# A graph kernel's first root product in three fp32r terms, and the last third of three roots between two neighbour sums

## The reference

```
out = x @ W_root + bias
for r in range(NUM_RELATIONS):
    out += (sum of x over the neighbours under relation r / max(degree_r, 1)) @ W_r
```

## Time and profile before

| | |
|---|---|
| median of 3 runs | 801.77 us (800.8 to 802.37) |
| the profiled execution's own time | 805.78 us |
| its span, first to last instruction | 804.0 us |
| mean granted TensorE clock | 0.997 |
| busy: TensorE, DVE, GpSimd, ScalarE | 770.6, 599.6, 490.8, 423.5 us |

### The profile page before, as it was taken

The page is one execution under the profiler, slowest core; times in us unless marked ns, Lnnn a source line. Parts: engine busy times, 40 slices in busy tenths (PEclk is TensorE's granted clock), DMA queues, the critical chain, the costliest instruction groups (busy, mean ns, idle before and its releaser), DMA issues.

```text
span 804.0 us, 10573 instructions
## 1 busy us (share of the span) xinstructions
PE 770.6 (96%) x4182; PEld 640.3 (80%) x4182; DVE 599.6 (75%) x664; ACT 423.5 (53%) x508; POOL 490.8 (61%) x243
## 2 busy tenths in 40 slices
PE   7999999999999999998989999999998999998998
PEld 4668995677666799667657569999998999985897
DVE  8967139999999630999999987555986498567454
ACT  6524456777774442777867734434541454253742
POOL 0534709899998374698999936741873177805500
PEclk9999999999999999999999999999999999999999
DMA  9136427767765463385668838554463445350001
GB/s 359 45 80 235 158 79 198 171 166 209 199 182 130 167 226 118 69 220 105 142 186 201 263 125 303 183 183 164 151 220 134 157 157 202 114 236 0 2 1 40
DMA packets 28585, 126.22 MB, mean 157 GB/s; under 512 B 4084, under 2 KB 6644, under 8 KB 28152
## 3 DMA queue, kind: packets, MB, share of 16 engines
q1 hardware_dynamic: 23240, 104.24, 39.1%
q0 software_dynamic: 4176, 15.21, 10.2%
q10 hardware_dynamic: 1120, 6.10, 2.0%
HBM read 100.63 MB, written 0.79 MB: 126 GB/s over the span
## 4 chain that ended last, share of the span: by engine, by line
PE 70%; DVE 15%; POOL 5%; ACT 4%; DMA 2%; issue 2%; DVEq 0%; SPq 0%; ACTq 0%
PE ps L1156 26%; PE ps L1122 12%; DVE prod L2054 8%; PE ps L1447 6%; PE ps L1187 5%; PE ps L1494 4%; PE ps L1669 3%; ACT prod L868 2%; DVE qi_t L2076 2%; PE ps L1314 2%; PE ps L1335 2%; POOL prod L646 1%; POOL w_lo L630 1%; PE ps L1737 1%; PE ps L1315 1%
## 5 line engine op out<-in xcount | busy, mean ns | idle before, releaser
L630 POOL TENSOR_TENSOR w_lo<-w_raw,w_hi 128x1536 fp32r<-128x1536 f32 x49 | 183.2, 3749 | 145.1 <-ACT w_hi L737 145.0
L2054 DVE TENSOR_TENSOR prod<-prod,ps 128x2048 f32<-128x2048 f32 x96 | 217.4, 2282 | 2.7 <-ACT prod L868 2.4
L868 ACT ACTIVATE prod<-ps 128x1024 f32<-128x1024 f32 x192 | 185.8, 1024 | 58.2 <-PE ps L1447 56.1
L646 POOL TENSOR_TENSOR prod<-prod 128x1024 f32<-128x1024 f32 x65 | 157.3, 2424 | 37.0 <-DVE prod L2054 36.0
L737 ACT ACTIVATE w_hi<-w_raw 128x1536 fp32r<-128x1536 f32 x60 | 88.9, 1487 | 119.9 <-PE ps L1156 109.4
L1447 PE MATMUL ps<-sel_pair,h_and_q 128*128 128x512 f32 x384 | 127.7, 445 | 13.0 <-ACT prod L868 12.1
L1156 PE MATMUL ps<-w_hi,yt_hi 128*128 128x384 f32 x480 | 123.5, 338 | 3.0 <-DVE w_lo L1928 3.0
L1156 PE MATMUL ps<-w_lo,yt_hi 128*128 128x384 f32 x480 | 122.6, 336 | 0.0
L1156 PE MATMUL ps<-w_hi,yt_lo 128*128 128x384 f32 x480 | 122.6, 336 | 0.0
L1122 PE MATMUL ps<-w_raw,h_t 128*128 128x384 f32 x312 | 106.5, 486 | 0.0
L1447 PEld LDWEIGHTS ps<-sel_pair,h_and_q 128*128 128x128 f32 x384 | 66.6, 189 | 48.3 <-ACT prod L868 23.9
(11 more groups left out here) (266 smaller groups left out, 1156.3 us busy)
## 6 DMA issues: line engine op xcount, KB each, us to landing
w_raw<-weights SPq DMA_DIRECT2D x105, 768.0 KB, 4.4
prod<-prod POOLq DMA_DIRECT2D x29, 512.0 KB, 5.2
wa_in<-weights SPq DMA_DIRECT2D x6, 768.0 KB, 5.8
w_gat<-weights SPq DMA_DIRECT2D x6, 768.0 KB, 8.1
w_query<-weights SPq DMA_DIRECT2D x3, 768.0 KB, 11.9
a_vec<-gat_vectors ACTq DMA_DIRECT2D x1, 2048.0 KB, 8.6
h_and_q<-stage_hi SPq DMA_DIRECT2D x20, 96.0 KB, 2.2
h_and_q<-stage_lo SPq DMA_DIRECT2D x20, 96.0 KB, 2.2
```

What stands on the lines that cost most here:

```text
L630: pool.tensor_tensor(Wl[:, j, :], raw_slab(U, 0, j), Wh[:, j, :], ALU.subtract).then_inc(w_lo_by_pool, 1)
L646: pool.tensor_tensor(v[:, 0], v[:, 0], v[:, 1], ALU.add).then_inc(folded_once, 1)
L868: act.activation(slot_view(s)[:, u], args.rearrange("p b (n l) -> p (b n) l", l=LH), ACT.Sigmoid).then_inc(sigmoid_ready, 1)
L2054: TT(slot_view(s), slot_view(s), query, ALU.mult).then_inc(products_ready, 1)
```

## The change

The first layer's root joins the roots in three terms. `SPLIT_ROOTS` names the layers; unit 1 is in `SPLIT`, and its low words are GpSimd's. In the setup GpSimd makes these three `w_lo` after `counts4_ready`, between the two halves of `SEL`. ScalarE makes unit 1's high copies around the norms, `root_hi` takes the place of `keep_turned`, and the high copies of unit 2 now stand all three ahead of the `yt_hi` of sum 1, in the first layer alone. On DVE `root_lo(0, 0)` stands between the adds of the count rest, `root_lo(0, 1)` behind them; its low words have a buffer of their own, `first_root_lo`. SP issues unit 2's second and third slab before the second spread of queries. On TensorE the last third of root t = 1 stands between sum 1 and sum 2 in the first, fourth and fifth layers (in the first it did before). The counts waited for in `turn_kept` are one less everywhere, since one copy is gone.

```
+SPLIT_ROOTS = [0, 3, 4]
+SPLIT = [UNIT[l] + v for l in range(LAYERS) for v in range(l not in SPLIT_ROOTS, RELATIONS[l] + 1)]
+ROOTS = [UNIT[l] for l in SPLIT_ROOTS if l > 0]
...
+        first_root_lo = sb("first_root_lo", [P, KC, N], F32R, g_off)
...  SyncE
             spread_queries(0)
+            load(2, js=(1, 2))
             spread_queries(1)
-            load(2, js=(1, 2))
...  GpSimd
+            pool.wait_ge(counts4_ready, 1)
             pool.wait_ge(selectors_set, 3)
+            w_lo(UNIT[0])
+            pool.wait_ge(w_lo_by_pool, LO_AT[UNIT[0], 0, 2])
             equal(SEL[64:128, :].rearrange("p (n l) -> p n l", l=LH), const_in[64:128, C_IOTA:C_IOTA + LH].unsqueeze(1),
...  ScalarE
             def relations(layer):
                 U = UNIT[layer]
+                if layer == 0:
+                    w_hi(U + 1)
                 yt_hi(layer, 1)
-                w_hi(U + 1, (1, 2))
+                if layer > 0:
+                    w_hi(U + 1, (1, 2))
...
-            w_hi(2, (0,))
+            w_hi(UNIT[0], (0, 1))
             for t in range(NT):
                 relu_norm(0, t, h_ready[t])
+            w_hi(UNIT[0], (2,))
             stage_queries(0, 0)
             act.wait_ge(counts4_ready, 1)
             copy(A4t[:], A4i[:]).then_inc(setup_counts_copied, 1)
-            keep_turned(0, 1)
+            root_hi(0, 0)
             stage_queries(1, 2)
+            root_hi(0, 1)
...  TensorE
                     turn(1, e)
-                    root(layer, 0, 4, KC)
-                if degrees is not None:
+                    root_part(layer, 0, 1)
+                    root_part(layer, 0, 2)
                     degrees()
                     pe.wait_ge(staged_lo, 2)
-                    root(layer, 1, 0, 4)
-                if layer > 2:
-                    for j in range(3):
+                if layer == 0 or layer > 2:
+                    for j in range(2):
                         root_part(layer, 1, j)
...
                     aggregate(layer, 1)
-                if layer < 3:
-                    root(layer, 1, 4 if degrees is not None else 0, KC)
+                    root_part(layer, 1, 2)
+                if layer in (1, 2):
+                    root(layer, 1, 0, KC)
                 aggregate(layer, 2)
...
-                pe.wait_ge(turn_kept[1], 1)
+                pe.wait_ge(root_lo_ready[1], 1)
...
             pe.wait_ge(staged_lo, 1)
-            root(0, 0, 0, 4)
+            root_part(0, 0, 0)
...  VectorE
             ch.step(TT(rest[:], A4i[:, :, 0, :], A4i[:, :, 1, :], ALU.add))
-            for a_, op in ((A4i[:, :, 2, :], ALU.add), (A4i[:, :, 3, :], ALU.add), (A3[:, :, 0, :], ALU.subtract)):
-                ch.step(TT(rest[:], rest[:], a_, op))
+            ch.step(TT(rest[:], rest[:], A4i[:, :, 2, :], ALU.add))
+            root_lo(0, 0)
+            ch.step(TT(rest[:], rest[:], A4i[:, :, 3, :], ALU.add))
+            ch.step(TT(rest[:], rest[:], A3[:, :, 0, :], ALU.subtract))
             TT(A3[:, :, 2, :], rest[:], A3[:, :, 1, :], ALU.subtract).then_inc(counts3_ready, 1)
             stage_rows(QUERY_EVENTS[1], 2)
-            keep_turned(0)
+            root_lo(0, 1)
```

More of the change, by code:

```diff
@@ L49 @@
 ORDER.append((30, 0))
-SPLIT = [UNIT[l] + v for l in range(LAYERS) for v in range(l < 3, RELATIONS[l] + 1)]
-ROOTS = [UNIT[l] for l in range(3, LAYERS)]
+SPLIT_ROOTS = [0, 3, 4]
+SPLIT = [UNIT[l] + v for l in range(LAYERS) for v in range(l not in SPLIT_ROOTS, RELATIONS[l] + 1)]
+ROOTS = [UNIT[l] for l in SPLIT_ROOTS if l > 0]
 SLOT, LANDED, PRIOR = {}, {}, {}
@@ L769, in root_hi @@
             def root_hi(layer, t):
-                act.wait_ge(turned[t], layer + 1 if t == 0 else INPUT[layer] + 1)
+                act.wait_ge(turned[t], layer + 1 if t == 0 and layer > 0 else INPUT[layer] + 1)
                 copy(YTh[:, 1, :, t * P:(t + 1) * P], chunk_tile(4 + 2 * t, KC)).then_inc(root_hi_ready[t], 1)
@@ L1142, in root_part, with three_terms @@
                 if j == 0:
-                    pe.wait_ge(root_lo_ready[t], layer - 2)
+                    pe.wait_ge(root_lo_ready[t], SPLIT_ROOTS.index(layer) + 1)
                     root_bias(layer, pair(layer, t))
                 wait_lo(pe, UNIT[layer], j)
-                mm = three_terms(1, j, t, pair(layer, t), False)
+                low = first_root_lo[:] if layer == 0 else YTl[:, 1]
+                mm = three_terms(YTh[:, 1], low, j, t, pair(layer, t), False)
                 if t == 1:
                     mm.then_inc(w_used, 1)
-            def three_terms(s, j, t, bank, last):
+            def three_terms(high, low, j, t, bank, last):
                 for k in (2 * j, 2 * j + 1):
-                    for n, (Y, Wx) in enumerate(((YTh, Wh), (YTh, Wl), (YTl, Wh))):
+                    for n, (Y, Wx) in enumerate(((high, Wh), (high, Wl), (low, Wh))):
                         for h in range(2):
                             c0 = (k % 2) * F + h * FH
-                            mm = pe.matmul(ps[:, bank + h, 0:FH], Y[:, s, k, t * P:(t + 1) * P], Wx[:, j, c0:c0 + FH],
+                            mm = pe.matmul(ps[:, bank + h, 0:FH], Y[:, k, t * P:(t + 1) * P], Wx[:, j, c0:c0 + FH],
                                            start=False, stop=(last and k == KC - 1 and n == 2))
@@ L1164, in root @@
                 if k0 == 0:
-                    pe.wait_ge(turn_kept[t], e + 1)
+                    pe.wait_ge(turn_kept[t], e)
                     root_bias(layer, bank)
@@ L1220, in last_of_first_aggregate @@
                 A = A3 if layer < 2 else A4
-                pe.wait_ge(turn_kept[1], INPUT[layer] + 1)
+                pe.wait_ge(turn_kept[1], INPUT[layer])
                 pe.wait_ge(yt_lo_ready, BEFORE[layer])
@@ L1237, in product, with layer_products @@
                 pe.wait_ge(yt_lo_ready, BEFORE[layer] + 3 * (v - 1) + (j + 1))
-                return three_terms(1 - v % 2, j, t, pair(layer, t), last)
-            def layer_products(layer, degrees=None):
+                return three_terms(YTh[:, 1 - v % 2], YTl[:, 1 - v % 2], j, t, pair(layer, t), last)
+            def layer_products(layer, degrees):
                 e, R = INPUT[layer], RELATIONS[layer]
@@ L1252, in layer_products @@
                         pe.wait_ge(half_kept, 2)
-                        pe.wait_ge(turn_kept[0], 5)
+                        pe.wait_ge(turn_kept[0], 4)
                         keep_clock(layer)
@@ L1273, in layer_products @@
                         pe.wait_ge(h_lo_ready[t], layer + 1)
-                    if layer == 0:
-                        pe.wait_ge(turn_kept[1], e + 1)
                     aggregate(layer, 1)
-                if layer < 3:
-                    root(layer, 1, 4 if degrees is not None else 0, KC)
+                    root_part(layer, 1, 2)
+                if layer in (1, 2):
+                    root(layer, 1, 0, KC)
                 aggregate(layer, 2)
@@ L1474, in bank7_free @@
                     if n == 0:
-                        pe.wait_ge(turn_kept[1], e + 1)
+                        pe.wait_ge(turn_kept[1], e)
                         return
@@ L1484, in bank7_free @@
                     if kind == "h" and m == 1:
-                        pe.wait_ge(turn_kept[0], INPUT[i + 1] + 1)
+                        pe.wait_ge(turn_kept[0], INPUT[i + 1])
                 def fold(at_):
@@ L1579, in beside @@
                         fold(s)
-                pe.wait_ge(turn_kept[0], e + 1)
+                pe.wait_ge(turn_kept[0], e)
                 first_heads(acc + 1, 0, P, 0, KC)
@@ L1601, in _ @@
             for layer in range(2, LAYERS):
-                layer_products(layer)
+                layer_products(layer, None)
             def transpose_tile(t, src, ready, count, chunks, bank):
@@ L1919, in root_lo @@
             def root_lo(layer, t):
-                dve.wait_ge(root_hi_ready[t], layer - 2)
+                dve.wait_ge(root_hi_ready[t], SPLIT_ROOTS.index(layer) + 1)
                 cols = slice(t * P, (t + 1) * P)
-                TT(YTl[:, 1, :, cols], chunk_tile(4 + 2 * t, KC), YTh[:, 1, :, cols], ALU.subtract).then_inc(root_lo_ready[t], 1)
+                low = first_root_lo[:] if layer == 0 else YTl[:, 1]
+                TT(low[:, :, cols], chunk_tile(4 + 2 * t, KC), YTh[:, 1, :, cols], ALU.subtract).then_inc(root_lo_ready[t], 1)
             def w_lo(U, j):
@@ L2041, in first_copy_query @@
                 def first_copy_query():
-                    dve.wait_ge(turn_kept[1], 2 * i + 2)
+                    dve.wait_ge(turn_kept[1], 2 * i + 1)
                     dve.tensor_copy(ps[:, 6, :].rearrange("p (f c) -> p f c", f=2), qTf[:, 0:2, 0:4 * L]).then_inc(query_copied, 1)
```

## The result

The changed kernel takes 805.4 us (median of 5 runs, 803.76 to 806.32), against 801.77 before. The ratio is 1.0044, with a 95% interval from 1.0032 to 1.0056. A second measurement, on another chip, gave 805.92 against 801.39 (1.0054, from 1.0041 to 1.0066). Forecast were 804.2 us and a range from 799.6 to 806.3.

A forecast was written before the change was run, and what follows sets the result against it. TensorE, busy 96% of the span, was taken as the bound. -2.99 + 2.6 + 2.83 - 1.90 = +0.54 us, plus 1.85 for the clock, made +2.4 on 801.77: 804.2 us, range 799.6 to 806.3.

The forecast's parts named there:

- the rival with both falls: First layer: both new TensorE waits lower the clock, +4.2 us, 806.0 us; chance 0.20.
- The root in three terms: First layer, TensorE: 72 matmuls in 12.49 us replace 24 plain f32 products in 15.48, saving 2.99 us.
- Layers four and five: The root's last third covers TensorE's wait for the scaled sums, 0.95 us in each layer, saving 1.90 us.
- the eleven microseconds of cover: Layers four and five: the next weight's delayed high copy stays hidden, needed only 2.84 + 8.3 us later.
- The adds held up by `w_lo`: First layer, DVE: count adds wait for GpSimd's w_lo, delaying root_lo(0, 0); TensorE waits 2.6 us before the root.
- ScalarE's order: First layer: the third high copy stands ahead of yt_hi, so TensorE waits 2.83 us before the second sum.
- The counts and the spread in time: First layer: later counts, 1 us to spare, and the queries' spread, narrowly hidden, cost TensorE nothing more.
- The clock: First layer: likeliest one new wait lowers the clock, +1.85 us, sized on the row with a 2.98 us wait.
- The faster rival: First layer: adds aren't held up, so no first wait; 799.7 us, or 801.6 with a lowered clock; chance 0.20.
- The gain given back: Layers four and five: a late w_hi or slab loses their gain, +1.9 on the forecast, 806.1 us; chance 0.07.
- The Trainium skill's rule for the comparison: First layer: GpSimd's comparison also holds up DVE's adds, root_lo(0, 1) is 2.0 us late, 806.2 us; chance 0.04.
- The profiled execution: Whole kernel: profiled 805.78 us would become about 808.2; the same difference was applied to the median 801.77.

The follow-up runs named there:

- e1: Changed kernel with ScalarE's third high copy of unit 2 put back behind the three yt_hi of the first sum: 801.3 us, 0.9992 of the kernel before.
- e2: Changed kernel with DVE's order alone changed, each root_lo ahead of later adds on the counts: 802.45 us, 1.0004 of the kernel before.
- e3: Changed kernel with both order edits, ScalarE's (e1) and DVE's (e2): 798.13 us, 0.9962 of the kernel before.
- e5: Changed kernel with 20 unread matmuls put into each of TensorE's two first-layer waits: 804.08 us, 1.0018 of the kernel before.
- e9: Kernel of e6 again, on the chip of e10: 797.25 us, 0.9945 of the kernel before.
- e10: Kernel of e4 again, on the chip of e9: 799.2 us, 0.9967 of the kernel before.
- e4: Kernel before with only the root's last third moved between the two sums in layers four and five: 798.92 us, 0.997 of the kernel before.
- e0: Kernel before, unchanged, profiled a second time: median 802.08 us, profiled span 798.1 us.
- e6: e3 plus the third slab's low words on DVE and ScalarE's root_hi of tile 1 before the second staging: 797.0 us, 0.9935 of the kernel before.
- e7: Changed kernel, unchanged, measured again on another chip: 805.92 us.

## Why the prediction was right, point by point

The sign, the range and the places were right, and the two waits came for the reasons given. The step that was mis-sized is the clock's: "likeliest is that one falls: +1.85". Two fell, at some 1.5 us each, so the time lies nearer to the rival with both falls (806.0) than to the forecast. The second sum's end shows it: 71.60 + 2.44 + 1.85 = 75.9 by the forecast, 78.16 measured. Of these 2.3 us, 1.2 are the second fall (two of 1.5 instead of one of 1.85), 0.5 the sum that starts behind a wait, which the forecast had at its usual 2.84, 0.3 the root's smaller saving, and 0.3 the bias and the first sum.

- **The root in three terms, -2.99 us.** 24 matmuls of it took 4.25 or 4.26 us at the full clock (in e1, e2, e3 and e5 alike), so 72 take 12.8: about 2.7 saved. It showed as a gain, 2.46 in the profile and 2.0 in the medians, only when the waits were gone (e9 against e10).
- **Layers four and five, -1.90.** -1.86 in the profile, and alone it made the kernel faster (e4, e10). No wait for a weight stands there, so the eleven microseconds of cover held.
- **The adds held up by `w_lo`.** The forecast had the first two end at 45.0 and 49.0 and TensorE start at about 50.0. They ended at 45.03 and 48.86, and TensorE started at 50.00. The wait was 3.22 us and not 2.6, because TensorE was free at 46.78 and not at 47.41. That moves the wait's start, not its end. The prediction took 47.41 from one profile, and that moment differed by up to 1.3 us between executions; that the forecast of this wait's cost fits the balance (2.59) owes something to the profile chosen. e2, which changes only the order on DVE, removed the wait.
- **ScalarE's order, 2.83 us.** 2.85. e1 removed it alone.
- **The counts and the spread in time.** Right for the changed kernel. As soon as the first wait was gone, the counts were 0.57 and 0.83 us late (e2, e3), behind a copy of ScalarE's that in the changed kernel doesn't stand in front of them.
- **The clock.** I gave the two waits a chance of somewhat over a half and of 0.7, and took one fall as likeliest. Two came, in seven of ten executions listed. This was the rival with 0.20 (806.0 us). The 2.98 us row was the near neighbour of both waits, 3.22 and 2.85, and that should have had more weight. e5 showed that the falls come from these waits, and e2 and e1 that each goes with its wait.
- **The faster rival** (adds not held up) is out by the rows above. **The gain given back** is out by e4. **The Trainium skill's rule for the comparison** was half right: see the last section.
- **The profiled execution.** I took its 4 us above the median for something that would stay the same. Most of it was a wait and a fall that most executions lack (e0). The sum was made of differences in other stages, so the forecast didn't suffer. That was luck: the two profiled spans (804.0 and 804.5) by themselves would have shown next to no change.

## What to carry to other kernels

When work moves to an engine that shares something with another, ask what that other engine has queued in the same stretch, and put what the busiest engine waits for ahead of it: here two adds nobody wanted yet stood before `root_lo`. A copy that waits for the busiest engine must not stand ahead of copies on which that engine waits; moving one instruction behind three was worth 4 us. Here a new wait of about 3 us on TensorE cost itself and 1.5 us of lowered clock. After each mended wait look for the next one: of the root's 2.7 us saved, 0.4 appeared with two waits mended and 2.46 with four. And take a second profile before you build on a moment read from the first.

## What the runs showed of the hardware

A GpSimd comparison (tensor_scalar, one SBUF input) held a DVE instruction with two SBUF inputs up as well, but in the instances here only at its beginning. GpSimd's row is first, DVE's second, in the kernel of e6:

```profile
48.72 3.17 POOL L674 TENSOR_SCALAR sel_pair<-const_in 64x1024 fp32r<-64x1024 f32 x1
```
```profile
49.20 2.56 DVE L1937 TENSOR_TENSOR w_lo<-w_raw,w_hi 128x1536 fp32r<-128x1536 f32 x1
```

DVE's `w_lo` takes 1.76 us by itself (at 615.35 in the kernel before). It ended at 51.76, so by my estimate it was let go near 50.1, 1.4 us after the comparison began and 1.8 before it ended. In e9 the same two instructions give 1.4 us again (comparison from 48.43, `w_lo` ended at 51.47). In the changed kernel the fourth add (L2024) ended at 54.26. Such an add ends 0.55 us after it is let go, which makes 53.7, 1.4 us after the comparison's start at 52.27. In the kernel before, the add at 41.77 came 1.8 us after the second comparison's start and wasn't held up. The Trainium skill, in "SBUF — State Buffer", section "Who interferes with whom", says that two SBUF inputs on DVE contend with any GpSimd instruction that reads SBUF. The trace agrees that they do, in these instances for the first 1.4 of 3.17 us; no run here varied the comparison to say why.

From 40 us on, the profiles compared here hold seven waits of TensorE of over 2 us: 2.98 in the kernel before, 3.22 and 2.85 in the changed one and 3.26 and 2.85 in its second profile (e7), 2.94 in e1 and 2.84 in e2. Behind each the granted clock was 0.50 in a stretch of at least 2 us.

The other surprise is the 6.7 us at 0.50 in e2, from within its wait of 2.84 us (it ended at 69.92) to 76.1. In the changed kernel the clock was at 1.0 again in the window from 78.0, after a wait of 2.85 us that ended at 73.31. TensorE was busy for 6.18 of e2's 6.7 us.
